# One chain for all scales of an attention step, and the v bias on VectorE

## The reference

```python
x = _ln(x, ln1_w, ln1_b)
qk = silu(x @ Wqk.T + bqk)                  # 64 columns
v = silu(x @ Wv.T + bv)                     # 512 columns
heads = qk[..., None, :] * gamma + beta     # four heads, each with rope
quad_q, lin_q, quad_k, lin_k = map(_rope, ...)
attn = relu(quad_q @ quad_k.T / G + bias) ** 2      # in groups of G = 64 tokens
lin_kv = lin_k.T @ v / n                            # over the whole batch
out = silu(x @ Wg.T + bg) * (attn @ v + lin_q @ lin_kv)
out = _ln(out @ Wo.T + bo, ln2_w, ln2_b)
x1 = _layernorm(x + out)
# experts: a shared one for all tokens, and 8 routed ones, top 2 of a softmax
y = gelu(x1 @ Wfc_s + b) @ Wproj_s + b + sum over the top 2 of gate * (the same with Wfc[e], Wproj[e])
return _layernorm(x1 + y)
```

## Time and profile before

| | us |
|---|---|
| median of three runs | 914.61 |
| the profiled execution | 913.94 |
| its span | 912.1 |
| PE busy | 882.9 |
| PE weight loads busy | 787.5 |
| DVE busy | 682.7 |
| ACT busy | 549.7 |
| POOL busy | 264.4 |

### The profile page before, as it was taken

How to read it: one execution, slowest core, us unless ns; L and a number is a source line. 1 busy time by engine, 2 the same in 40 slices (tenths; PEclk the granted TensorE clock), 3 DMA queues, 4 the chain that set the end, 5 groups by cost and what they waited for, 6 DMA issues and landing times.

```text
span 912.1 us, 17238 instructions
## 1 busy us (share of the span) xinstructions
PE 882.9 (97%) x5744; PEld 787.5 (86%) x5744; DVE 682.7 (75%) x1686; ACT 549.7 (60%) x1015; POOL 264.4 (29%) x186
## 2 busy tenths in 40 slices
PE   4999999999999999999999999999999999999995
PEld 3788788788788789899999999999999999999985
DVE  7688889889978599676576675757655579997475
ACT  5546656666646755556556455555545568887475
POOL 0000011001010047338535255543535345542000
PEclk9999999999999999999999999999999999999998
DMA  5142224223226424529665474855676558886723
GB/s 168 52 154 75 85 76 138 75 75 115 75 89 211 170 49 82 134 93 266 151 202 128 152 225 98 248 144 169 152 239 179 145 132 231 230 227 191 239 70 115
DMA packets 70126, 133.35 MB, mean 146 GB/s; under 512 B 14334, under 2 KB 55095, under 8 KB 62776
## 3 DMA queue, kind: packets, MB, share of 16 engines
q1 hardware_dynamic: 49864, 107.68, 35.6%
q0 software_dynamic: 16512, 21.32, 13.9%
q10 hardware_dynamic: 3696, 3.67, 1.2%
HBM read 98.13 MB, written 33.46 MB: 144 GB/s over the span
## 4 chain that ended last, share of the span: by engine, by line
PE 52%; DVE 7%; issue 2%; DMA 2%; ACT 1%; POOL 0%; DVEq 0%; ACTq 0%; SPq 0%; POOLq 0%
PE bank L1719 23%; PE bank L1794 22%; PE bank L1739 3%; PE bank L1745 3%; DVE s_hl L1632 2%; DMA k_wstage<-wall 2%; PE bank L1779 1%; DMA residual_sums<-s_y,s_dest 1%; POOL residual_sums L1178 0%; DVE s_mst L1584 0%; PE bank L1817 0%; DVE s_wpj0l L1529 0%; DVE s_wfc0l L1529 0%; ACT s_h L1314 0%; ACT s_hh L1318 0%
## 5 line engine op out<-in xcount | busy, mean ns | idle before, releaser
L1314 ACT ACTIVATE s_h<-bank,k_bfc 128x512 f32<-128x512 f32 (+1 forms) x216 | 134.4, 622 | 196.4 <-PE bank L1794 187.4
L1632 DVE TENSOR_TENSOR s_hl<-s_h,s_hh 128x512 fp32r<-128x512 f32 (+1 forms) x206 | 124.9, 607 | 133.0 <-ACT s_hh L1318 132.1
L1178 POOL DMA_INDIRECT residual_sums<-s_y,s_dest x64 | 108.5, 1696 | 183.4 <-DVE s_y L1562 170.0
L1318 ACT ACTIVATE s_hh<-s_h 128x512 fp32r<-128x512 f32 (+1 forms) x216 | 122.9, 569 | 9.1
L1794 PE MATMUL bank<-k_uh,s_wfc0h 128*128 128x512 f32 (+1 forms) x384 | 120.2, 361 | 0.0
L1719 PE MATMUL bank<-k_wpj1l,s_hh 128*128 128x256 f32 x384 | 108.6, 283 | 2.1 <-DVE s_hl L1632 2.1
L1719 PE MATMUL bank<-k_wpj1h,s_hh 128*128 128x256 f32 x384 | 108.0, 281 | 0.0
L1719 PE MATMUL bank<-k_wpj1h,s_hl 128*128 128x256 f32 x384 | 107.9, 281 | 0.0
L1719 PE MATMUL bank<-s_wpj0l,s_hh 128*128 128x256 f32 x344 | 96.7, 281 | 0.5 <-DVE s_hl L1632 0.4
L1719 PE MATMUL bank<-s_wpj0h,s_hh 128*128 128x256 f32 x344 | 96.5, 281 | 0.0
L1719 PE MATMUL bank<-s_wpj0h,s_hl 128*128 128x256 f32 x344 | 96.4, 280 | 0.0
(11 more groups left out here) (341 smaller groups left out, 2228.8 us busy)
## 6 DMA issues: line engine op xcount, KB each, us to landing
k_wstage<-wall SPq DMA_DIRECT2D x42, 1024.0 KB, 6.0
s_acc<-wall SPq DMA_DIRECT2D x14, 1024.0 KB, 7.8
s_x_res<-x SPq DMA_DIRECT2D x8, 512.0 KB, 4.7
x_rows<-s_x SPq DMA_DIRECT2D x8, 512.0 KB, 3.6
residual_sums<-s_x SPq DMA_DIRECT2D x8, 512.0 KB, 4.3
x_parts<-s_x1h SPq DMA_DIRECT2D x8, 512.0 KB, 2.6
x_parts<-s_x1l SPq DMA_DIRECT2D x8, 512.0 KB, 3.7
k_uh<-x_parts SPq DMA_DIRECT2D x8, 512.0 KB, 5.6
```

The source lines that it names most:

```text
L1178: pool.indirect_dma_start(RES, bass.IndirectOffsetOnAxis(dest[:, at:at + 1].bitcast(U32), 0), y[:, t, :], None, bounds_check=N + S - 1, co ...
L1314: nc.scalar.activation(h[j % 2][:, cols], b[:, cols], ACT.Gelu_apprx_tanh, bias=bfc[w][:, j:j + 1]).then_inc(h_ev, 1)
L1318: nc.scalar.activation(hh[j % RING][:, cols], h[j % 2][:, cols], ACT.Copy).then_inc(hh_rd, 1)
L1632: tt(hl[j % RING][:, cols], h[j % 2][:, cols], hh[j % RING][:, cols].bitcast(F32), ALU.subtract).then_inc(hl_rd, 1)
```

## The change

1. The bias of v: PE's product L771 goes, and with it the tile bv2. DVE adds a tile bv_all, which holds the bias row in all 128 partitions, to each of the four banks and writes v; ACT then applies Silu in place.
2. The chains: in steps 1 to 7 the scales of z, of x_in and of the o result are worked out in one chain of 12 columns (8 in step 1) behind the o statistics. The o result is centred into the tile qkr instead of z. ACT's norms of x1 and xn move between the second and third gate Silu; query_low stands ahead of the o statistics; the scores are squared between centring and scaling.
3. PE: all att x v products first, then the linear ones.
4. The start: 40 products of the tile bo2 with itself while PE waits for the first xn, 8 more behind the first transposes; step 0 takes its x_in statistics behind the heads and query_low; its v products with the low weights come last in each tile.
5. SP issues lq and the reload of x_in ahead of the x1 stores.
6. Experts: POOL also takes the low parts of (1, 1) and (1, 2).

```diff
-        bv2 = sb("bv2", [P, E], F32R)
+        bv_all = sb("bv_all", [P, E])
...
-            load(ld_c0, (raw_bv, a["rows"][:, 0, :]), (raw_bo[:, :], a["rows"][:, 1, 0:D]), (ones_raw[:, :], a["ones"]))
+            load(ld_c0, (bv_all[:, :], a["rows"][0:1, 0, :].to_broadcast([P, E])), (raw_bo[:, :], a["rows"][:, 1, 0:D]), (ones_raw[:, :], a["ones"]))
...
-                    for t in range(TT):
-                        act.wait_ge(v_mm, 4 * b + t + 1)
-                        nc.scalar.activation(v[:, t, :], bank[t][:, :], ACT.Silu).then_inc(v_ev, 1)
                 if not is_int(b) or b >= 3:
                     act.wait_ge(lg_mm, b - 2)
                     copy(logits[:, bass.ds((b - 3) * TT, TT), :], bank[7][:, :].rearrange("p (t n) -> p t n", t=TT)[:, :, 0:2 * NE]).then_inc(lg_ev, 1)
-                if last:
+                if main:
+                    for t in range(TT):
+                        act.wait_ge(v_biased, 4 * b + t + 1)
+                        nc.scalar.activation(v[:, t, :], v[:, t, :], ACT.Silu).then_inc(v_ev, 1)
+                def sums_normed():
                     act.wait_ge(scale_rd, b + 2)
                     need(act, x1_st, 32 * (b - 2))
-                    normed(x1, z, TT, x1_rd)
+                    normed(x1, z, SUM, x1_rd)
+                if last and not main:
+                    sums_normed()
+                def ahead_normed():
+                    act.wait_ge(scale_rd, b + 2)
+                    act.wait_ge(xT_mm, 2 * b + 2)
+                    normed(xn, x_in, 0, xn_ready)
                 if main:
...
                     else:
+                        queries()
                         keys()
                         for m in range(KE):
+                            if last and m == 2:
+                                sums_normed()
+                            if ahead and m == 2:
+                                ahead_normed()
                             act.wait_ge(g_mm, 4 * b + m + 1)
                             nc.scalar.activation(u[:, m, :], bank[m][:, :], ACT.Silu,
...
+            weights_hi(1)
             act.wait_ge(ld_v0, 32)
             x_transposed(0, (0,))
-            for n in (1, 2, 3):
-                weights_hi(n)
+            weights_hi(2)
             steps(act, step, end=B + 3)
...
                 main, ahead, o, last = stages(b)
                 at = lambda n: is_int(b) and b == n
                 c = b - 2
+                merged = main and not at(0)
                 if last:
                     dve.wait_ge(res_used, c + 1)
-                    stats([z[:, t, :] for t in range(TT)], TT)
-                if ahead:
+                    stats([z[:, t, :] for t in range(TT)], SUM)
+                def ahead_stats():
                     dve.wait_ge(ld_x, 16 * (b + 1))
                     stats([x_in[:, t, :] for t in range(TT)], 0)
...
+                if merged and ahead:
+                    ahead_stats()
+                if last and not main:
+                    need(dve, x1_rd, c)
+                    moments(nc, link, st[:, SUM:, :], mean[:, SUM:], var[:, SUM:], tmp[:, SUM:])
                     if at(B + 1):
                         beside(4)
-                    rsqrt(nc, link, rs[:, now], half[:, now], var[:, now], tmp[:, now])
-                    shifts(now.start, now.stop)
+                    rsqrt(nc, link, rs[:, SUM:], half[:, SUM:], var[:, SUM:], tmp[:, SUM:])
+                    shifts(SUM, SUM + TT)
                 if at(B + 1):
                     beside(5)
...
+                if main:
+                    need(dve, u_mm, 4 * b)
                     for t in range(TT):
...
+                        dve.wait_ge(v_mm, 4 * b + t + 1)
+                        tt(v[:, t, :], bank[t][:, :], bv_all[:, :], ALU.add).then_inc(v_biased, 1)
+                def query_low():
                     dve.wait_ge(lqh_rd, b + 1)
                     tt(qkr[QK:P, 1, :], heads[QK:P, 0, :], lq[QK:P, :].bitcast(F32), ALU.subtract).then_inc(lql_rd, 1)
-                    if is_int(b) and b == 0:
-                        dve.wait_ge(ld_c, 16 * CONSTS)
+                def scores_squared():
...
+                if at(0):
+                    query_low()
+                    ahead_stats()
+                    rstd(0, TT)
+                    shifts(0, TT)
+                if o:
+                    yo = [bank[6 + t // 2][:, t % 2 * D:t % 2 * D + D] for t in range(TT)]
+                    dve.wait_ge(ld_r, 16 * b)
+                    tt(x_res[:, :, :], x_res[:, :, :], ln2[:, 1:2, :].to_broadcast([P, TT, D]), ALU.add).then_inc(res_rd, 1)
+                    if merged:
+                        query_low()
+                    stats(yo, OUT, lambda t: t % 2 or dve.wait_ge(o_mm, 2 * (b - 1) + t // 2 + 1))
+                    now = slice(0 if ahead else OUT, SUM + TT if merged and last else SUM)
+                    if merged:
+                        need(dve, xn_ready, min(b, B - 1) + 1 if is_int(b) else b + 1)
+                        if last:
+                            need(dve, x1_rd, c)
+                    moments(nc, link, st[:, now, :], mean[:, now], var[:, now], tmp[:, now])
+                    if at(B):
+                        beside(0)
+                    rsqrt(nc, link, rs[:, now], half[:, now], var[:, now], tmp[:, now])
+                    if merged:
+                        shifts(now.start, now.stop)
+                    if at(B):
+                        beside(1)
+                        x1_rest()
+                    centred = qkr[:, :, :].rearrange("p s (h d) -> p (s h) d", d=D) if merged and last else z
+                    if merged and last:
+                        dve.wait_ge(lq_rd, 16 * b + 16)
+                    elif last:
+                        dve.wait_ge(x1_rd, c + 1)
+                    for t in range(TT):
+                        stt(centred[:, t, :], yo[t], mean[:, OUT + t:OUT + t + 1], ln2[:, 0, :], ALU.subtract, ALU.mult).then_inc(o_ev, 1)
+                    if at(B):
+                        beside(2)
+                    if merged:
+                        scores_squared()
+                    dve.wait_ge(o_ev, 4 * b)
+                    dve.wait_ge(res_rd, b)
+                    if merged and last:
+                        dve.wait_ge(x1_rd, c + 1)
+                    for t in range(TT):
+                        last_i = stt(z[:, t, :], centred[:, t, :], rs[:, OUT + t:OUT + t + 1], x_res[:, t, :], ALU.mult, ALU.add)
+                    last_i.then_inc(res_used, 1)
+                if at(B):
+                    beside(3)
+                if main:
+                    if at(0):
+                        dve.wait_ge(ld_c, 16 * CONSTS)
+                        scores_squared()
                     dve.wait_ge(kv_ev, b + 1)
                     stt(kvl[:, :], bank[6][:, :], 1.0 / T, kvh[:, :].bitcast(F32), ALU.mult, ALU.subtract).then_inc(kvl_rd, 1)
                 if ahead:
@@ -639,13 +698,13 @@
                     tt(ul[:, m, :], u[:, m, :], uh[:, m, :].bitcast(F32), ALU.subtract).then_inc(ul_rd, 1)
                 if main:
+                    if last:
+                        x1_rest()
                     for m in range(KE):
                         dve.wait_ge(u_mm, 4 * b + m + 1)
                         tt(u[:, m, :], u[:, m, :], bank[1 + m][:, :], ALU.mult).then_inc(u_ml, 1)
                         if m:
                             rest(m - 1)
-                        elif last:
-                            x1_rest()
                     rest(KE - 1)
                 elif at(B + 1):
...
             weights_lo(0)
+            dve.wait_ge(ld_c0, 48)
+            nc.vector.tensor_copy(ones2[:, :], ones_raw[:, :])
+            dve.wait_ge(zeroed, 1)
...
+            dve.wait_ge(warm, 2)
             bias_rows(bo2[0:BR, :], raw_bo[:, :])
...
-                        mm(bank[t][:, :], ones2[:, :], bv2[:, :], start=True, stop=False)
                         for k in range(KD):
                             last_i = three(bank[t][:, :], xTh[:, k, cols], xTl[:, k, cols], wv[0][:, k, :], wv[1][:, k, :],
-                                           False, k == KD - 1)
+                                           k == 0, k == KD - 1)
                         last_i.then_inc(v_mm, 1)
...
                 if main:
-                    pe.wait_ge(kvl_rd, b + 1)
-                    pe.wait_ge(lq_rd, 16 * b + 16)
                     for m in range(KE):
                         if m < 3:
                             pe.wait_ge(g_ev, 4 * b + m + 2)
                         elif last:
                             pe.wait_ge(x1T_ev, 2 * c + 1)
                         rows = slice(m * P, (m + 1) * P)
-                        out = bank[1 + m]
-                        mm(out[:, :], kvh[:, rows], lq[:, :], start=True, stop=False)
-                        mm(out[:, :], kvl[:, rows], lq[:, :], start=False, stop=False)
                         for t in range(TT):
```

(20 more changed lines are left out.)

113 lines of the change are left out of this document (50 added, 63 removed).

## The result

Six runs of the changed kernel took 925.0 to 930.35 us, median 928.25; six of the one before, in the same comparison, 915.86. The ratio is 1.0135, 95% interval 1.0122 to 1.0147: slower by 1.35%. The forecast was 913.0, its range 903.5 to 919.5.

The account below looks back on a forecast made before the run. PE was taken to bound the kernel, exactly full in a steady step, DVE having 10% to spare. Start -2.0, step 1 -0.5, steps 2 to 7 +0.9, rest 0: -1.6, 912.3; 0.67 to the median: 913.0 us, range 903.5 to 919.5.

Parts of the forecast that it names:

- The first qk product: Start of step 0: with idle products ahead, it comes at 11.8 us instead of 14.34.
- the gate wait: Step 0, gate's first product: PE waits 3 to 4 us, since v goes through an addition behind the heads.
- query_low held by POOL: Steps 2 to 7: DVE's query_low overlaps POOL's weight operation and loses 1.4 to 1.86 us, 1.7 on average.
- q+20.9: Time after a step's first qk product (q) at which PE, unhindered, wants the kv product.
- the first rival: The saving is kept: DVE passes query_low ahead of POOL, kv wait 0 to 0.3 us, 904.0 to 905.6; chance 0.36.
- With it PE waits 1.7 - 0.5 = 1.2 us at the kv product: Steps 2 to 7: POOL's hold of 1.7 less 0.5 slack makes PE wait 1.2 us for bank 6.
- the experts' 2: Experts: three held DVE operations, a wait of about 2 us for the choices likely; net taken as 0, up to +3.
- not 0.8: Step 1: 0.8 us of wait for about 2 us of one-time DVE work; net -0.5.
- The logits wait of step 8: Last steps: one longer wait for the logits and 0.9 us less work, together taken at 0.
- The product order: Each step: att x v products together pay the opening pair's extra about once, saving 4 x 0.08 = 0.3 us.
- The 0.2 for bank 4: Steps 2 to 7: att x v product into bank 4 comes earlier against ACT's copy of x1T, costing 0.2 us.
- The rival *Slower: ACT's norms of x1 and xn come late and PE waits at the transposes, 0.8 a step; median 919.8; chance 0.17.

Follow-up runs that it names:

- Experiment 2: Changed kernel with POOL's weight operation of steps 2 to 7 released by the second v product, not the last o product: 918.36 us, ratio 1.0038.
- Experiment 1: Changed kernel with idle PE products ahead of kv (steps 1 to 7), step 0's first gate product and step 8's logits transposes: 922.9 us, ratio 1.0076.
- experiment 8: Changed kernel with earlier POOL release, POOL's old share, step 0's v additions and one-time DVE work moved, idle products ahead of step 8's logits transposes: 907.27 us.
- experiment 10: Kernel of experiment 8 with POOL's share of the experts' low parts as in the change, from (1, 1) on: 911.27 us, ratio 0.9941.
- experiment 11: Kernel of experiment 8 with the v bias on PE (32 products) and not on DVE: 912.69 us, ratio 0.9954.
- experiment 12: Kernel of experiment 8 without the 48 idle products at the start: 909.09 us, ratio 0.9931.
- experiments 4: Changed kernel with POOL's share of the experts' low parts as before the change, from (1, 3) on: 928.68 us, ratio 1.0128.
- idle_start: Kernel before the change plus 40 idle products in PE's first wait and 8 behind the first transposes: 913.6 us, ratio 0.9985.
- experiments 5 to 7: Kernel before with one part each: att x v products first, 923.18 us; idle products at the start, 913.6; v bias as DVE additions, 954.53.

## Why the prediction was wrong

**What held.** The places and much of the mechanism. The first qk product (11.8, measured 11.86), the gate wait (3 to 4, 4.12), query_low held by POOL (2 or more, 2.08 to 2.79), PE ready for kv at q+20.9 (20.92), and a kv wait from DVE's centring in steps 2 to 6. Step 7 went as the first rival had it: DVE passed query_low ahead of POOL and PE didn't wait. Experiment 2 confirms the mechanism: take the hold away and the wait goes. But the period was 34.0 to 34.6 in steps 3 to 5, over the 33.4 to 33.9 of the forecast.

**The step that failed: "With it PE waits 1.7 - 0.5 = 1.2 us at the kv product", and that such a wait costs its length.**

1. The prediction charged a wait with its length. It counted the low clock as a matter of the start alone. At six of the new waits PE ran at the lower level, for some 3.4 us at five of them, 1.7 us lost each, and for longer at the choices: about 11 of the 16.4 us between the two profiled runs, where the forecast was -1.6. Experiment 1 gives back 5.3 us in the medians. The forecast's own waits would not have brought the time out of the range by this alone. In no profile did a low stretch follow a wait as short as 1.2 us (the list is in the last section), so of the eight new waits only the gate's 4 us and perhaps the experts' 2 would have had one: 913.0 + 1.7 to 3.4 = 914.7 to 916.4, by estimate. It took the longer waits of point 2 as well. The rows of before showed the price, 0.41 instead of 0.233 behind the first wait, and I did not carry it to the waits that I forecast.
2. The wait was 1.86 and not 1.2 in step 4. The laying out was short by 0.25 where query_low starts (14.45 for 14.2), by 0.15 in the hold, and by 0.25 in the chain (3.47 from the end of the statistics to the centring, for 3.2). At the wait these sums of small terms are the result, since they stand behind a slack of only 0.5. In step 1 it was 2.65, not 0.8: I took about 2 us of one-time DVE work and didn't lay out its row. With that work inside step 0 and the v additions of step 0 ahead of the heads (experiment 8) the wait is gone. The logits wait of step 8, 2.79 instead of 1.13, I had put at nothing together with the work saved there.
3. The product order saves 0, not 0.3 a step (5.42 against 5.39). The 0.54 for a pair behind f32 products was read rightly, but the att x v products behind it take 0.81 and not 0.89, so the pair costs nothing more. The 0.2 for bank 4 was not there either: the 32 att x v products of step 4 stand 0.11 to 0.12 apart throughout.
4. The experts were +4.3 and not 0: five held operations instead of three (experiment 10: 4.0 us), and some 2.6 of the 4.3 is the low clock behind the wait, which is counted in point 1 as well.
5. The rival *Slower* named ACT's norms as the decider. They were not: no wait for xn is in the list behind the start. The place where its price came from was wrong, so that its time (919.8) was the nearest of the cases is luck, and its sign, a period over 34.4, was seen in step 4 (34.55) without its cause.

The gain that the change could have given was real. Experiment 8 is 8.4 us faster than the kernel before, where the forecast had 9.0 to 10.7 for the saving kept. The bias products' 0.93 a step came to 0.5 to 0.7 in steps 3 to 6 (experiment 11), since DVE still holds kv up a little. The idle products gave 2.0 on the kernel before (0.9985 [0.9973, 0.9997]); in experiment 12 they can't be told from nothing.

What stays open: why the clock fell behind some waits and not behind others of the same length (below), and why step 1's kv wait was 1.1 shorter in experiment 1. The number of low stretches differs from run to run, and I can't tell how many the unprofiled runs had.

## What to carry to other kernels

Where PE is full, first price a new wait at its length plus, if it comes near 2 us, what the lower clock costs behind it (1.7 us here), and look for idle products to fill it; where there is no wait they cost their own length (1.7 us in step 7 of experiment 1). Then ask what makes the wait. Before giving work to the engine with 10% to spare, lay out its row up to the point where the full engine needs it, and look which operation of two SBUF inputs will now stand beside a POOL operation: releasing POOL's work by another semaphore was worth 10 us here. Judge a part of a change in a kernel without other new waits; in the changed kernel itself a loss of 4 us (experiments 4 and 10) was not to be seen.

## What the runs showed of the hardware

In the profiled runs of all these kernels, each of PE's 23 waits of 2.5 us and more behind the first qk product had a stretch at 0.50 in it or close behind it, and none of those from 1.0 to 1.75 us had. Of the waits from 1.77 to 2.03 us eleven had one and seven had not. So two waits of the same kind and length can differ in what follows. Windows behind the wait of 2.0 us for s_hl in experiment 8's kernel, and behind that of 1.98 in experiment 4's:

```profile
312.30:314.30 2.00, 1.94 (x13) 1.94 (x14) 1.90 (x5) 1.32 (x2) 0.00 (x0) 0.82 0.03 8
314.30:316.30 2.00, 2.00 (x7) 1.52 (x6) 1.93 (x7) 0.00 (x0) 0.58 (x1) 0.50 0.00 0
316.30:318.30 2.00, 2.00 (x15) 1.90 (x14) 1.93 (x5) 1.32 (x2) 1.40 (x1) 0.83 0.00 0
```

```profile
334.10:336.10 2.00, 1.97 (x14) 1.90 (x15) 1.90 (x4) 1.32 (x2) 0.00 (x0) 1.00 0.00 0
336.10:338.10 2.00, 1.81 (x10) 1.27 (x9) 1.93 (x7) 0.66 (x1) 0.61 (x1) 1.00 0.00 0
```

The same holds for the kv waits: 1.88 in step 6 and 1.94 in step 2 had the low clock behind them, 1.86 in step 4 did not, and in experiment 4's profile it stood behind 1.89 in step 4 and not behind 1.89 in step 6. In idle_start's kernel (experiments 5 to 7) the first qk product waited 2.15 and the products behind it stood 0.23 apart. The spread of the times within a kernel is of the size of one such stretch or two, which fits but is not shown for the runs without a profile: the changed kernel's runs lie at 925 to 927 (clock 0.989 to 0.990) and at 930 (0.984 to 0.985).
